# Cross attentions: scores for the maxima three heads earlier, rounding of q and k one pair earlier

## The chip, the core and the metric

The kernel runs on one core of a Trainium2 chip. The core has five engines with a queue each: PE (matrix products, with PEld as its weight loads), DVE (vectors), ACT (activations), POOL (GpSimd) and SP, which here only issues DMAs. Each queue is worked off in the order in which it was written; engines wait for each other on semaphores. The metric is the device time of one execution in microseconds, lower is better.

## The reference, cut to what matters

A decoder of two layers over x (64 sequences, 64 tokens, 256 channels). Stage by stage: a RWKV mixer, a banded cross attention with a context, a ternary MLP, a causal attention, a second cross attention without weights, and a mixture of experts. The change touches the two cross attentions alone. The first is:

```python
qkv = x @ w_in.T + b_in            # per sequence, 64 channels x 256 positions
scores = jnp.einsum('bqhd,bkhd->bhqk', q, k) / jnp.sqrt(jnp.asarray(d, q.dtype))
scores = jnp.where(band[None, None], scores, neg)      # |i - j| <= 64
attn = jax.nn.softmax(scores, axis=-1)
o = jnp.einsum('bhqk,bkhd->bqhd', attn, v).reshape(n, t, e)
o = o @ w_out.T + b_out
y = jax.nn.relu(o) * encodings
out = jnp.einsum('nit,io->not', y, w_ct) + b_ct[None, :, None]
```

The second has no projections, no band and no gate: its queries are the normalised x, its keys and values are the context itself, in 8 heads of 8 channels over 256 positions.

## The kernel before

`wide_attention` (L292) builds both cross attentions; `banded` tells the first from the second. Two sequences form a pair, so there are 32 pairs of 16 heads: heads 0 to 7 are those of the first sequence (s = 0), 8 to 15 of the second (s = 1). Each engine has one function `step(p, u, first, last)` that is written out 32 times, once per pair, with a loop over the heads j = 0 to 15 in it. Buffers alternate with the pair's parity u. What one head j of step p holds on PE:

- `make_scores_t` (L488, in the first attention with L491, which adds the band): transposed scores of pair p, two heads ahead (RING = 2). ACT takes their exponentials (L747).
- `make_scores` (L475): scores of pair **p + 1**, head j, for the row maxima alone. DVE takes the maxima (L617 in the first, L621 in the second). A score needs the maxima of two heads before it, as its bank in PSUM is shared by every second head.
- `multiply` (L506) at odd j, `align` (L516) of pair p - 1 at j = 4, and the small products of the first attention: `project` (L525, L526: q and k of pair p + 2) at j = 2, `make_values` (L535, in the second L541) at j = 5, `gate_product` (L554) at 10, `out_product` (L558) at 13.

The maxima go back into the transposed scores as three more rows of q. POOL splits them into three bf16 parts (`split_maxima`, L827 to L833), PE turns them (`turn_maxima`, L549: s = 1 of pair p at j = 1, s = 0 of pair p + 1 at j = 9), ACT copies them (`keep_maxima`, L780), and SP stores them with one DMA (`place_maxima`, L437: `xattn_qp<-xattn_mrow`). `make_scores_t` of heads 0 and 8 waits for that DMA (`rows_in`).

q and k are rounded to bf16 in three parts: ACT (`round_1`, L770), POOL (`left_overs`, L818), ACT (`round_2`, L774), POOL (L820). In step p this is done for pair p + 2, from j = 2 or 3 on. SP writes the parts to HBM (`store`, L416 and L420, six DMAs) and reads them back in the layout of the scores (`place`, L432, four DMAs for each s). SP's order in step p is: place_maxima(p, 1), store(p + 2), place(p + 2, 0), place_maxima(p + 1, 0), place(p + 2, 1), load_context. What sets each engine's order is the order of these calls in the code; nothing reorders it.

## Time and profile before

| | us |
|---|---|
| median of 3 runs | 2892.37 (2889.06 to 2894.8) |
| profiled execution, own time | 2875.17 |
| its span | 2873.3 |
| first cross attention: first to last score for the maxima | 391.7 to about 1098 |
| second cross attention: the same | 1869 to 2447 |
| PE busy over the span | 2247.8 (78%) |
| DVE, ACT, POOL busy over the span | 1850.9 (64%), 1165.6 (41%), 896.5 (31%) |

The page gives one profiled execution. In a timeline a row is: start, duration, engine, line, operation, output and inputs; a bracket at its end gives the time that the engine was idle before it and what ended that.
### The profile page before, as it was taken

How to read it: one execution, taken by the hardware profiler on the slowest of the kernel's cores; microseconds unless marked ns; L12 is line 12 of the kernel's file. 1: busy time of each engine (PE TensorE's matmuls, PEld its weight loads, DVE VectorE, ACT ScalarE, POOL GpSimd, SP SyncE). 2: the span in 40 equal slices, each digit the busy share in tenths (PEclk: the TensorE clock that was granted, in tenths of full speed). 3: DMA queues.
4: the chain of work that ended last, by engine and by line, in shares of the span. 5: the costliest groups of instructions: out<-in, count | busy, mean ns of one | idle time of the engine just before them, and what ended most of it. 6: DMA issues, size and time to landing. Idle time of an engine off the chain costs nothing. (4 is left out here: it accounts for less than half of the span.)

```text
span 2873.3 us, 55107 instructions
## 1 busy us (share of the span) xinstructions
PE 2247.8 (78%) x19084; PEld 1596.6 (56%) x19084; DVE 1850.9 (64%) x5654; ACT 1165.6 (41%) x2616; POOL 896.5 (31%) x1488
## 2 busy tenths in 40 slices
PE   4777658888888885599986999478888888549886
PEld 3666535555555553599975777334444444425553
DVE  4999956766666666655543666467777777415345
ACT  1222224444444443222224666246565655313222
POOL 3555622222222121466660000212222222143522
PEclk9888769999999897799997999779999999669998
DMA  3000042333223330000003000343333433022434
GB/s 106 1 1 0 1 114 74 85 79 81 74 74 85 78 82 4 1 2 2 2 16 130 2 2 1 109 93 101 92 102 93 102 92 86 7 83 76 145 119 155
DMA packets 252306, 183.17 MB, mean 64 GB/s; under 512 B 29056, under 2 KB 246304, under 8 KB 251264
## 3 DMA queue, kind: packets, MB, share of 16 engines
q1 hardware_dynamic: 240416, 156.52, 20.6%
q0 software_dynamic: 7456, 18.92, 1.8%
q10 hardware_dynamic: 4160, 4.19, 0.5%
q8 instruction: 157, 2.57, 0.4%
q14 instruction: 117, 0.96, 0.1%
HBM read 94.47 MB, written 83.51 MB: 62 GB/s over the span
## 5 line engine op out<-in xcount | busy, mean ns | idle before, releaser
L747 ACT ACTIVATE xattn_pr<-ps 128x384 f32<-128x384 f32 (+1 forms) x1024 | 536.6, 543 | 467.5 <-PE ps L491 281.8
L488 PE MATMUL ps<-xattn_qp,xattn_kp 128*128 128x192 bf16 (+1 forms) x2048 | 428.8, 270 | 93.6 <-DMA xattn_qp<-xattn_mrow 92.7
L475 PE MATMUL ps<-xattn_kp,xattn_qp 96*128 96x192 bf16 (+1 forms) x2048 | 386.7, 272 | 78.3 <-DVE xattn_mx L621 32.9
L621 DVE TENSOR_REDUCE xattn_mx<-ps 128x2 f32<-128x512 f32 x512 | 335.7, 677 | 154.1 <-PE ps L475 148.2
L506 PE MATMUL ps<-xattn_pr,xattn_vs 128*32 128x256 f32 (+1 forms) x4096 | 318.6, 384 | 19.9 <-ACT xattn_o L752 19.8
L617 DVE CUSTOM_DVE_ANT_0 xattn_masked<-ps,xattn_band 128x192 bf16<-128x192 f32 x1024 | 325.2, 354 | 8.4 <-issue 5.8
L488 PEld LDWEIGHTS ps<-xattn_qp,xattn_kp 128*128 128x128 bf16 x2048 | 189.5, 100 | 242.8 <-DMA xattn_qp<-xattn_mrow 120.2
L475 PEld LDWEIGHTS ps<-xattn_kp,xattn_qp 96*128 96x128 bf16 x2048 | 189.2, 102 | 133.6 <-DVE xattn_mx L621 54.7
L491 PE MATMUL ps<-xattn_band,xattn_ident 128*128 128x192 bf16 x1024 | 225.6, 259 | 0.0
L978 PE MATMUL ps<-ffn_parts,gate_up_t 128*128 128x128 bf16 x3072 | 194.4, 221 | 2.1 <-DVE ffn_parts L1096 2.1
L978 PEld LDWEIGHTS ps<-ffn_parts,gate_up_t 128*128 128x128 bf16 x3072 | 184.2, 98 | 16.3 <-DVE ffn_parts L1096 2.5
L615 DVE MEMSET xattn_tick<- 128x1 f32 x512 | 30.2, 59 | 227.2 <-PE ps L475 221.1
L1580 PE MATMUL ps<-expert_gu,moe_xbt 128*128 x312 | 157.4, 629 | 8.1 <-issue 4.2
L1806 DVE SCALAR_TENSOR_TENSOR moe_tg<-moe_tanh,ps 128x256 f32<-128x256 f32 x78 | 32.8, 421 | 195.5 <-ACT moe_tanh L1661 195.5
L506 PEld LDWEIGHTS ps<-xattn_pr,xattn_vs 128*32 128x32 f32 x4096 | 83.5, 110 | 120.9 <-issue 83.1
L992 PE MATMUL ps<-proj_t,ffn_h 128*128 128x256 f32 x512 | 138.7, 394 | 0.5 <-DVE ffn_h L1087 0.5
L818 POOL TENSOR_TENSOR xattn_rest<-xattn_qk,xattn_parts 128x512 f32<-128x512 f32 x64 | 74.0, 1156 | 206.7 <-ACT xattn_parts L770 206.7
L198 POOL TENSOR_TENSOR xattn_rs<-x_stat,const_sb 128x1 f32<-128x1 f32 x64 | 12.2, 190 | 395.9 <-DVE x_stat L193 395.9
L638 DVE RECIPROCAL xattn_rden<-ps 128x128 f32<-128x128 f32 x128 | 120.9, 947 | 22.0 <-PE ps L516 22.0
L1873 POOL DMA_INDIRECT moe_rows_out<-rwkv_w,moe_to x78 | 75.2, 964 | 185.2 <-DVE rwkv_w L1816 174.5
L827 POOL TENSOR_TENSOR xattn_mparts<-xattn_mx,const_sb 128x16 bf16<-128x16 f32 x128 | 27.6, 216 | 330.7 <-DVE xattn_mx L621 242.2
L1049 ACT ACTIVATE ffn_tanh<-ps 128x256 f32<-128x256 f32 x128 | 49.1, 383 | 195.4 <-PE ps L978 195.4
(304 smaller groups left out, 4736.7 us busy)
## 6 DMA issues: line engine op xcount, KB each, us to landing
xattn_rows<-xattn_parts SPq DMA_DIRECT2D x128, 192.0 KB, 2.1
xattn_qp<-xattn_rows SPq DMA_DIRECT2D x256, 96.0 KB, 2.9
xattn_kp<-xattn_rows SPq DMA_DIRECT2D x256, 96.0 KB, 3.2
xattn_rows<-xattn_parts SPq DMA_DIRECT2D x128, 128.0 KB, 2.1
moe_rows_in<-region_zero SPq DMA_DIRECT2D x6, 1677.0 KB, 7.3
moe_xb<-moe_rows_in SPq DMA_DIRECT2D x78, 129.0 KB, 2.1
xattn_rows<-xattn_parts SPq DMA_DIRECT2D x128, 64.0 KB, 1.8
moe_row<-moe_rows_out SPq DMA_DIRECT2D x16, 512.0 KB, 8.3
```

The source lines that it names most:

```text
L475: mm = nc.tensor.matmul(ps[:, BANK_S + j % RING, mt * D:mt * D + width], qp[u][s][0:R_MAX, h, mt * P:(mt + 1) * P], kp[u][s][0:R_MAX, h, l ...
L488: mm = nc.tensor.matmul(out, kp[u][s][:, h, nt * P:(nt + 1) * P], qp[u][s][:, h, lo:lo + width], start=True, stop=not banded)
L491: mm = nc.tensor.matmul(out, ident16[:], band16[:, nt, :], start=False, stop=True)
L506: mm = nc.tensor.matmul(out, vs[u][:, QUAD * g + t, nt, :], pr[(QUAD * t + g) % (2 * QUAD)][:, nt, q], start=first, stop=(t % 2 == 1 and n ...
L617: ins = nc.vector.tensor_tensor_reduce(out=masked[:, mt, :], in0=ps[:, BANK_S + j % RING, mt * D:mt * D + WIN], in1=band16[:, mt, :], scal ...
L621: ins = nc.vector.tensor_reduce(mx[s][:, h * NT:(h + 1) * NT], ps[:, BANK_S + j % RING, :].rearrange("p (m n) -> p m n", m=NT), AX.X, ALU.max)
L638: nc.vector.reciprocal(rden[:, x], ps[:, BANK_N, D + half * P:D + (half + 1) * P]).then_inc(normal, 1)
L747: nc.scalar.activation(out, src, ACT.Exp, scale=HD ** -0.5).then_inc(exped, 1)
L978: mm = nc.tensor.matmul(ps[:, BANK_G + j % 2, o:o + P], w(j, n % NT, ft), row, start=(n == 0), stop=(n == len(rows) - 1))
L992: mm = nc.tensor.matmul(ps[:, bank, 0:D], h[j % 2][:, ft * P:(ft + 1) * P], down_w(j, ft), start=start and ft == 0, stop=stop and ft == 1)
L1580: mm = nc.tensor.matmul(ps[:, BANK_G + n % 2, :], xbt[n % 2][:, kt, :], gu[:, kt, bass.ds(e, 1), :].rearrange("p a f -> p (a f)"), start=( ...
L1873: g.indirect_dma_start(y_out[part], bass.IndirectOffsetOnAxis(ap=to[n % RB][:, 0:1], axis=0), yb[n % RB], None,).then_inc(sent[n % RB], 16)
```

## The change

1. `make_scores` and the maxima on DVE run three heads further ahead (LEAD = 3): step p makes heads 3 to 15 of pair p + 1 and heads 0 to 2 of pair p + 2. Pair 1's first three stand before the steps.
2. The maxima are turned and kept one head earlier: s = 1 at j = 0, s = 0 at j = 8.
3. Normalising, projecting and rounding q and k in step p are for pair p + 3, not p + 2, and stand later in the step: `project` at j = 10 in place of 2, `round_1` and `round_2` at 11 and 13 (second attention: 7 and 9) in place of 3 and 5 (2 and 4). Storing and placing remain for pair p + 2. Pair 2 is rounded before the steps.
4. `make_values` moves from j = 5 to j = 3, DVE's `values` from 7 to 4, `normalise_q` from 0 to 5 (second: 3), `reciprocal_sums` from 5 and 6 to 6 and 7.
5. POOL splits s = 0 of pair p + 1 first, then makes the left overs, then splits s = 1 of pair p + 1; `reciprocal_std` stays last. On SP `load_context` of the second attention stands behind the six stores, and a wait on `placed` two pairs back is added before them.

```diff
+    LEAD = 3
@@ store, on SP
                     sp.wait_ge(left_over, 2 * (p + 1))
+                    for s in range(S2):
+                        if p >= 2:
+                            sp.wait_ge(placed[u][s], by_parity(p - 2, u, 64))
@@ step, on SP
-                    if not banded and there(p + 2):
-                        load_context(p + 2, u)
                     place_maxima(p, u, 1)
                     if there(p + 2):
                         store(p + 2, u)
+                    if not banded and there(p + 3):
+                        load_context(p + 3, 1 - u)
+                    if there(p + 2):
                         place(p + 2, u, 0)
...
@@ project and make_values, on PE
-                    wait(pe, vo_ready, p - 1)
                     wait(pe, qk_ready, p)
-                    wait(pe, max_kept, run(p - 1, 0))
+                    wait(pe, max_kept, run(p - 2, 0) + 1)
...
-                    if not banded:
-                        wait(pe, max_kept, run(p, 0))
+                    wait(pe, max_kept, run(p, 0))
...
@@ step, on PE
-                        if not last:
-                            make_scores(p + 1, 1 - u, j)
+                        ahead = next_head(p + 1, 1 - u, j + LEAD)
+                        if there(ahead[0]):
+                            make_scores(*ahead)
...
-                        if j == 1:
+                        if j == 0:
                             turn_maxima(p, 1)
-                        if banded and j == 2 and there(p + 2):
-                            project(p + 2, u)
+                        if not last and j == 3:
+                            make_values(p + 1, 1 - u)
+                        if not last and j == 8:
+                            turn_maxima(p + 1, 0)
+                        if banded and j == 10 and there(p + 3):
+                            project(p + 3, 1 - u)
...
+                if banded:
+                    project(2, 0)
+                for j in range(LEAD):
+                    make_scores(1, 1, j)
                 for j in range(RING):
                     make_scores_t(0, 0, j)
@@ step, on DVE
-                        if not last:
-                            maxima(p + 1, j)
-                        if j == 0 and there(p + 2):
-                            normalise_q(p + 2, u)
-                        if j in (5, 6) and not first:
-                            reciprocal_sums(p - 1, j - 5)
-                        if j == 7 and not last:
+                        ahead = next_head(p + 1, 1 - u, j + LEAD)
+                        if there(ahead[0]):
+                            maxima(ahead[0], ahead[2])
+                        if j == 4 and not last:
                             values(p + 1, 1 - u)
+                        if j == (5 if banded else 3) and there(p + 3):
+                            normalise_q(p + 3, 1 - u)
+                        if j in (6, 7) and not first:
+                            reciprocal_sums(p - 1, j - 6)
@@ step, on ACT
-                        if j == 1:
+                        if j == 0:
                             keep_maxima(p, u, 1)
                         if j == 2 and not first:
                             keep_o(p - 1)
-                        if there(p + 2):
-                            if banded and j == 2:
-                                projections(p + 2, u)
-                            if j == (3 if banded else 2):
-                                round_1(p + 2, u)
-                            if j == (5 if banded else 4):
-                                round_2(p + 2)
-                        if j == 9 and not last:
+                        if j == 8 and not last:
                             keep_maxima(p + 1, 1 - u, 0)
+                        if there(p + 3):
+                            if banded and j == 10:
+                                projections(p + 3, 1 - u)
+                            if j == (11 if banded else 7):
+                                round_1(p + 3, 1 - u)
+                            if j == (13 if banded else 9):
+                                round_2(p + 3)
@@ step, on POOL
-                    split_maxima(p, 1)
-                    if there(p + 2):
-                        left_overs(p + 2, u)
                     if not last:
                         split_maxima(p + 1, 0)
+                    if there(p + 3):
+                        left_overs(p + 3, 1 - u)
+                    if not last:
+                        split_maxima(p + 1, 1)
                     if not first:
                         fin.reciprocal_std(nc, g, p - 1)
```

What now stands in a row, at three places. PE, first attention, heads 2 and 3 of a step, before: the scores for the maxima of head 2, the two projections, head 3, and the first four products with the values (`pr` are the exponentials, `vs` the values).

```order
L475 MATMUL ps<-xattn0_kp00,xattn0_qp00 128x192 x2
L525 MATMUL ps<-xattn0_xn1,wide_q 128x256
L526 MATMUL ps<-xattn0_xn1,wide_k 128x256
L488 MATMUL ps<-xattn0_qp10,xattn0_kp10 128x192
L491 MATMUL ps<-xattn0_band16,xattn0_ident16 128x192
L488 MATMUL ps<-xattn0_qp10,xattn0_kp10 128x192
L491 MATMUL ps<-xattn0_band16,xattn0_ident16 128x192
L475 MATMUL ps<-xattn0_kp00,xattn0_qp00 128x192 x2
L506 MATMUL ps<-xattn0_pr0,xattn0_vs1 32x256
```

The same engine with the change, heads 10 and 11 of a step (line numbers shift: L483 is `make_scores`, L496 and L499 `make_scores_t`, L532 and L533 the projections, L562 `gate_product`, L514 `multiply`).

```order
L483 MATMUL ps<-xattn0_kp01,xattn0_qp01 128x192 x2
L532 MATMUL ps<-xattn0_xn0,wide_q 128x256
L533 MATMUL ps<-xattn0_xn0,wide_k 128x256
L562 MATMUL ps<-xattn0_on,wide_out 128x256
L496 MATMUL ps<-xattn0_qp11,xattn0_kp11 128x192
L499 MATMUL ps<-xattn0_band16,xattn0_ident16 128x192
```

The projections have left the place between heads 2 and 3, ahead of the products that wait for ACT's copy of o, and stand behind head 10.

ACT, first attention, before: `keep_maxima` at head 1, then the copy of o (L752), the projections' copies and the first rounding among the exponentials.

```order
L780 ACTIVATE xattn0_mrow1<-ps 48x128
L747 ACTIVATE xattn0_pr4<-ps 128x2x192
L752 ACTIVATE xattn0_o<-ps 128x512
L758 ACTIVATE xattn0_qk0<-ps,wide_b_q 128x256
L759 ACTIVATE xattn0_qk0<-ps,wide_b_k 128x256
```

ACT with the change, heads 10 to 13 of a step and on to head 0 of the next (L775 and L776 copy the projections, L787 and L791 round, L764 are exponentials, L797 is `keep_maxima`).

```order
L775 ACTIVATE xattn0_qk0<-ps,wide_b_q 128x256
L776 ACTIVATE xattn0_qk0<-ps,wide_b_k 128x256
L764 ACTIVATE xattn0_pr5<-ps 128x2x192
L787 ACTIVATE xattn0_parts<-xattn0_qk0 128x2x256
L764 ACTIVATE xattn0_pr6<-ps 128x2x192
L764 ACTIVATE xattn0_pr7<-ps 128x2x192
L791 ACTIVATE xattn0_parts<-xattn0_rest 128x2x256
L764 ACTIVATE xattn0_pr0<-ps 128x2x192
L764 ACTIVATE xattn0_pr1<-ps 128x2x192
L764 ACTIVATE xattn0_pr2<-ps 128x2x192
L797 ACTIVATE xattn0_mrow1<-ps 48x128
```

The rounding now ends three exponentials ahead of the keeping of the later half's maxima.

POOL, first attention, before: the split of s = 1, the two left overs (L818, L820), and the split of s = 0.

```order
L833 TENSOR_TENSOR xattn0_mparts<-xattn0_mrest,xattn0_mparts 128x16
L818 TENSOR_TENSOR xattn0_rest<-xattn0_qk1,xattn0_parts 128x512
L820 TENSOR_TENSOR xattn0_parts<-xattn0_rest,xattn0_parts 128x2x256
L827 TENSOR_TENSOR xattn0_mparts<-xattn0_mx0,const_sb 128x16
L829 TENSOR_TENSOR xattn0_mrest<-xattn0_mx0,xattn0_mparts 128x16
```

POOL with the change: the left overs (L839, L841) come right before the split of s = 1 (`mx1`, from L848 on), and `reciprocal_std` (L198, L200) behind it.

```order
L839 TENSOR_TENSOR xattn0_rest<-xattn0_qk1,xattn0_parts 128x512
L841 TENSOR_TENSOR xattn0_parts<-xattn0_rest,xattn0_parts 128x2x256
L848 TENSOR_TENSOR xattn0_mparts<-xattn0_mx1,const_sb 128x16
L850 TENSOR_TENSOR xattn0_mrest<-xattn0_mx1,xattn0_mparts 128x16
L852 TENSOR_TENSOR xattn0_mparts<-xattn0_mrest,const_sb 128x16
L854 TENSOR_TENSOR xattn0_mparts<-xattn0_mrest,xattn0_mparts 128x16
L198 TENSOR_TENSOR xattn0_rs<-x_stat,const_sb 128x1
```

The left overs changed sides: they stood ahead of the split of s = 0 and stand now ahead of that of s = 1.

## Rows read from the trace of the kernel before

**Rows 1.** PE's waits, first attention, 420 to 1100: total us, times, longest.

```profile
PE ps L488 <- DMA xattn_qp<-xattn_mrow: 65.1, 30, 4.2
PE ps L549 <- POOL xattn_mparts L833: 26.7, 51, 1.7
PE ps L475 <- DVE xattn_mx L617: 21.4, 43, 0.9
PE ps L506 <- ACT xattn_o L752: 0.5, 1, 0.5
```

**Rows 2.** PE's waits, second attention, 1900 to 2450.

```profile
PE ps L475 <- DVE xattn_mx L621: 31.3, 60, 0.6
PE ps L488 <- DMA xattn_qp<-xattn_mrow: 26.3, 24, 5.6
PE ps L506 <- ACT xattn_o L752: 17.4, 30, 0.6
PE ps L549 <- POOL xattn_mparts L833: 9.3, 32, 0.5
```

**Rows 3.** SP's issues in one step of the first attention: start, us, line.

```profile
728.73 1.46 SPq L416 DMA_DIRECT2D xattn_rows<-xattn_parts  x3
...
733.45 1.36 SPq L432 DMA_DIRECT2D xattn_qp<-xattn_rows  x2
...
735.83 0.76 SPq L437 DMA_DIRECT2D xattn_qp<-xattn_mrow  x1
```

**Rows 4.** PE's timeline, the wait that ends this chain.

```profile
738.44 0.26 PE L488 MATMUL ps<-xattn_qp,xattn_kp 128*128 128x192 bf16 x1 [2.24 <-DMA xattn_qp<-xattn_mrow]
```

**Rows 5.** Windows: us; busy of PE, PEld, DVE, ACT, POOL; PEclk; DMA; GB/s.

```profile
432.68:1082.97 650.29, 542.95 (x5277) 369.32 (x5275) 432.14 (x2638) 304.34 (x665) 140.72 (x348) 0.94 0.32 79
...
740.00:743.00 3.00, 3.00 (x24) 1.70 (x20) 2.81 (x18) 0.98 (x2) 1.60 (x6) 0.50 0.29 36
```

**Rows 6.** PE's timeline, first attention: aligns of pairs 0, 4, 5, 29, a wait.

```profile
432.68 1.92 PE L516 MATMUL ps<-xattn_o,const_sb 128*128 128x256 f32 x8
...
521.66 1.92 PE L516 MATMUL ps<-xattn_o,const_sb 128*128 128x256 f32 x8
...
535.16 0.26 PE L488 MATMUL ps<-xattn_qp,xattn_kp 128*128 128x192 bf16 x1 [1.47 <-DMA xattn_qp<-xattn_mrow]
...
543.19 1.92 PE L516 MATMUL ps<-xattn_o,const_sb 128*128 128x256 f32 x8
...
1082.97 1.92 PE L516 MATMUL ps<-xattn_o,const_sb 128*128 128x256 f32 x8
```

**Rows 7.** PE's timeline, second attention: aligns of pairs 0, 11, 14, 29.

```profile
1909.65 1.89 PE L516 MATMUL ps<-xattn_o,const_sb 128*128 128x256 f32 x8
...
2110.17 1.89 PE L516 MATMUL ps<-xattn_o,const_sb 128*128 128x256 f32 x8
...
2161.79 1.89 PE L516 MATMUL ps<-xattn_o,const_sb 128*128 128x256 f32 x8
...
2435.00 1.89 PE L516 MATMUL ps<-xattn_o,const_sb 128*128 128x256 f32 x8
```

**Rows 8.** Groups by line over the whole span: count, busy us, mean ns.

```profile
L818 POOL TENSOR_TENSOR xattn_rest<-xattn_qk,xattn_parts 128x512 f32<-128x512 f32 x64 | 74.0, 1156 | 206.7 <-ACT xattn_parts L770 206.7
...
L770 ACT ACTIVATE xattn_parts<-xattn_qk 128x512 bf16<-128x512 f32 x64 | 40.6, 634 | 37.5 <-DMA xattn_qk<-in_ctx 27.0 <-DMA xattn_rows<-xattn_parts 10.4
...
L541 PE MATMUL ps<-const_sb,xattn_qk 128*128 128x128 f32 x64 | 14.2, 305 | 25.8 <-DMA xattn_qk<-in_ctx 25.8
```

**Rows 9.** POOL's timeline, one split of maxima, first and last operation.

```profile
730.59 0.21 POOL L827 TENSOR_TENSOR xattn_mparts<-xattn_mx,const_sb 128x16 bf16<-128x16 f32 x1 [1.89 <-DVE xattn_mx L617]
...
731.48 0.22 POOL L833 TENSOR_TENSOR xattn_mparts<-xattn_mrest,xattn_mparts 128x16 bf16<-128x16 f32 x1
```

**Rows 10.** DVE's normalising, first attention: ns shortest, median, longest.

```profile
L170 DVE TENSOR_SCALAR xattn_xn<-x_now,x_stat x32: 407/410/1965, 372.1 to 1057.5; 128x256 f32<-128x256 f32 x32
```

**Rows 11.** POOL's timeline at the start of the first attention.

```profile
372.01 7.60 POOL L845 MEMSET xattn_kp<- 128x2048 bf16 x4 [4.80 <-POOLq L206]
```

More of the change, by code:

```diff
@@ L460, in _ @@
                         place(p, p, s)
+                if not banded:
+                    load_context(2, 0)
                 place_maxima(0, 0, 0)
@@ L528, in make_values @@
                 def make_values(p, u):
-                    if not banded:
-                        wait(pe, max_kept, run(p, 0))
+                    wait(pe, max_kept, run(p, 0))
                     if banded:
-                        pe.wait_ge(qk_ready, p + 2 if there(p + 1) else p + 1)
+                        if p == 0:
+                            pe.wait_ge(qk_ready, 2)
                         for nt in range(NT):
@@ L548, in turn_maxima @@
                         pe.wait_ge(vo_ready, p + 1)
+                    elif banded and there(p + 2):
+                        pe.wait_ge(qk_ready, p + 3)
                     nc.tensor.transpose(ps[:, BANK_PREP, 0:P // 2].bitcast(BF16), mparts[:], ident16[:]).then_inc(max_turned, 1)
@@ L572, in step @@
                             align(p - 1)
-                        if j == 1:
+                        if j == 0:
                             turn_maxima(p, 1)
-                        if banded and j == 2 and there(p + 2):
-                            project(p + 2, u)
+                        if not last and j == 3:
[4 more added lines that the diff above has]
+                            project(p + 3, 1 - u)
                         if banded and not first and j == 10:
                             gate_product(p - 1)
-                        if not last and j == 5:
-                            make_values(p + 1, 1 - u)
                         if banded and not first and j == 13:
                             out_product(p - 1)
-                        if not last and j == 9:
-                            turn_maxima(p + 1, 0)
                 if banded:
@@ L727, in _ @@
                 values(0, 0)
+                normalise_q(2, 0)
                 for j in range(NHS):
                     maxima(0, j)
+                for j in range(LEAD):
+                    maxima(1, j)
                 over(v, PAIRS, step)
@@ L805, in _ @@
                 keep_maxima(0, 0, 0)
+                if banded:
+                    projections(2, 0)
+                round_1(2, 0)
+                round_2(2)
                 a.wait_ge(preset, 3)
@@ L850, in _ @@
                 split_maxima(0, 0)
+                left_overs(2, 0)
+                split_maxima(0, 1)
                 over(g, PAIRS, step)
```

## The prediction

> **What bounds the kernel now.** I read the waits of PE first, since the two cross attentions fill most of the profile's costly groups and PE is the engine with the largest busy time in both. In the first attention PE waits 65.1 us in 30 pairs for the DMA that stores the maxima's rows, 26.7 us for POOL's split of the maxima, 21.4 us for DVE's maxima, and once for ACT's copy of o [rows 1]. In the second the same list is shorter: 31.3 us for DVE, 26.3 for the DMA, 17.4 for the copy of o, 9.3 for the split [rows 2].
>
> Next, who makes that DMA late. The SP queue shows it: in one step the six stores of the rounded parts start at 728.73, the placing that has to wait for them to land at 733.45, and only behind it, at 735.83, the DMA of the maxima's rows [rows 3]. PE gets its rows at 738.44 after 2.24 us of idle time [rows 4]. The last operation of the split that belongs to this DMA started at 731.48 [rows 9], so the data was ready over 3 us before it could be issued: SP's queue is the cause, and what holds the queue is the rounding of q and k in the same step.
>
> Third, the pace. The reader counts from one align to another. In the first attention 29 periods lie between 432.68 and 1082.97: 650.29 / 29 = 22.42 us each [rows 6]. The granted clock is 0.94 over that stretch, against 0.50 (1.2 GHz) for 740 to 743, right behind the wait that ends at 738.44 [rows 4, 5]. A pair without such a stretch is 521.66 to 543.19, 21.53 us with a DMA wait of 1.47 in it [rows 6]. In the second attention 29 periods take 525.35 / 29 = 18.12 us, and the three from 2110.17 to 2161.79, in which PE hardly waited for the DMA, 51.62 / 3 = 17.21 [rows 7].
>
> **First attention, per pair.** Start from 21.53. (a) The rows' DMA: the store of pair p + 2 now finds its parts rounded a whole pair ago, so SP issues it right behind the maxima of head 0 instead of at a late left over. The six stores take about 3 us of issue, the first placing has to wait for head 5's transposed scores anyway, and the maxima of the earlier half are asked for at head 8 with SP's queue empty. From there to head 14 there are six heads, some 8 us at 21.53 / 16 = 1.35 each, for an issue and a landing that took 738.44 - 735.83 = 2.6 us [rows 3, 4]. The wait goes: -1.47. What is late next is not SP but the split of the later half, (c). (b) Half-speed stretches: 22.42 - 21.53 = 0.89 per pair is the clock and the longer DMA waits that come with it; the one in rows 5 begins behind such a wait, as those elsewhere in the stretch that I followed, so I let it go too. (c) The split: before, it cost PE 26.7 / 30 = 0.89 per pair in two waits. The earlier half's is made three heads before it is turned, so that one goes. The later half's stands behind the left overs of p + 3 on POOL, which stand behind ACT's second rounding at head 13. From that rounding: 0.63 (ACT) + 1.16 (POOL) + the split, 731.48 + 0.22 - 730.59 = 1.11, is 2.9 us [rows 8, 9]; it begins some 1.6 us into head 13 because the first left over (1.16) must be done, and PE reaches the turning at head 0 about 3.7 us after head 13 began. 1.6 + 2.9 - 3.7 = about 0.7 stays. That estimate is the weak one; nothing (0) and twice it (1.5) bound it. (d) DVE: the reciprocals come one head later and values leaves that stretch for head 4, so the queue of DVE behind the align is as long as before; I take 0.5 at heads 9 and 10, against 21.4 / 30 = 0.71 now. The wait at head 1 is covered by the turning's. (e) A new wait: in the first attention PE waited for ACT's copy of o once, because the projections of pair p + 2 stood between heads 2 and 3 and filled that time. They are gone to head 10. In the second attention, which never had them, the wait is 17.4 / 30 = 0.58 in each pair [rows 2]. I charge +0.58.
>
> Sum: 21.53 - 1.47 = 20.06; the split's 0.89 and DVE's 0.71 are in it on average, and that pair has them as 0.44 + 0.70 and 0.42 + 0.67, that is 2.23; 20.06 - 2.23 = 17.83 of work; + 0.7 + 0.5 + 0.58 = **19.6**. Against 22.42 that is -2.8 x 29 = **-82**. Bounds: with new waits of 1.0 in all 18.8 (-105), with all the old small waits kept beside the new one 20.6 (-53).
>
> **Second attention, per pair.** No projections, so no (e). The clean pace is 17.21; -0.91 against 18.12 is what the DMA wait is worth. But from the align to the score of head 13 DVE works without a break, and PE waits for it at heads 9 and 13 (31.3 / 30 = 1.04 per pair) [rows 2]. DVE loses values there and keeps maxima, reciprocals and the new x, and starts on the reciprocals a head later, so the score of head 13 comes as long after the align as before. The two transposes of make_values (L541, 0.305 each, overlapping to about 0.3) stood inside this stretch and cost nothing; at head 3 they stand ahead of the align and are on the path: +0.3 [rows 8]. The earlier half's split wait (9.3 / 30 = 0.31) lay in the same stretch and gives nothing back. 17.21 + 0.3 = **17.5**, -0.6 x 29 = **-18**. Bounds 17.0 (-32) and 18.3 (+5). Rounding at heads 7 and 9 needs the context that SP now loads behind the stores, at about head 4; it needs about 3 us to land and ACT asks at head 7, so this is just covered.
>
> **Ends of the stages.** In the first attention the longest DMA wait, 4.2 us in the first step, and its half-speed stretch go [rows 1]; against that pair 2 is rounded before the first exponentials: two roundings and two left overs, 2 x 0.63 + 2 x 1.16 = 3.6 [rows 8], and a split of 1.1, about +5. The second has a wait of 5.6 to lose [rows 2] and pays the same chain less what its own first maxima hide. I take -3 and -7: **-10**. The added wait on SP (placed, two pairs back) is for DMAs that landed a pair ago and what is queued behind it, six stores, never feels it; its cost is 0. The other stages keep their code.
>
> **Sum.** -82 - 18 - 10 = -110. Against the profiled execution that is 2875.17 - 110 = 2765; its time lies 17.2 below the median, and against the median of 2892.37 it is **2782**.
>
> **A rule that speaks against it.** DVE's normalising of one tile takes 0.407 us at the shortest and 1.965 at the longest [rows 10]; the long ones begin at 372.1, while POOL runs four memsets of 7.60 / 4 = 1.9 each [rows 11]. So a DVE operation can be held for a whole POOL operation. The Trainium skill says so in "SBUF — State Buffer", section "SBUF: two separate sides": DVE and GpSimd share one pair of ports as an exclusive lock, which also concerns DVE operations with two inputs in SBUF, and the loser waits for the whole instruction. By that rule, the trace agrees for memsets; no row shows it for the left overs, which stood beside no such DVE operation. Leaving it out gives 2782, and rival 1 is what it would make of the same sum.
>
> **Rivals.**
> 1. *DVE held by the left overs.* In the second attention the new x (two inputs in SBUF) is due at head 10 in DVE's unbroken stretch, and the second left over now follows a rounding at head 9. If it is hit in every pair, 1.16 x 29 = 34 us come back: 2782 + 34 = 2816. For: rows 10 and 11. Against: by the sums above the left over ends just before the new x begins, and an operation that starts second on POOL costs DVE nothing. 0.12.
> 2. *The half-speed stretches stay.* If they have another cause than the DMA waits, 0.89 x 29 = 26 us stay: 2808. For: the clock also fell behind waits of under 2 us. Against: at 740 the fall stands right behind a wait of 2.24, and with those gone the waits left are those of 0.6 and less that the clean pairs have too. 0.10.
> 3. *The change doesn't do what it says*: the rows' wait moves to head 6, since the later half's DMA stands behind the placing that waits for head 13's transposed scores. Then only the clock, the split and the ends move: of 82 + 18 about 35 remain, 2892 - 45 = 2847. Against: that placing takes about 2 us and is over before head 0. 0.08.
> 4. *Slower: the later half's chain lies bare.* At head 0 PE waits for the two copies of the projections (each of half a rounding's elements, so 0.63 together, an estimate from rows 8), rounding (0.63), left over (1.16), rounding, left over and split (1.11): 5.3 us if ACT gets to none of it while PE works on heads 10 to 15. Then it is (5.3 - 0.7) x 29 = 133 more, 2782 + 133 = 2915. It decides from a wait of 0.7 + 110 / 29 = 4.5 us. For: exponentials stand between all of these on ACT. Against: ACT is busy 304 of 650 us [rows 5]. 0.06.
>
> **How the numbers follow.** Forecast 0.60, between about 2760 and 2806; rivals 0.12, 0.10, 0.08, 0.06; 0.04 for a still larger gain. The range takes in the forecast, rivals 1 and 2 and the bounds of the first attention as far as they are likely: 2752 to 2828, 0.82. A measurement of this kernel can tell about 0.2% (5.8 us) from no change. Faster: 0.60 + 0.12 + 0.10 + 0.08 + 0.01 = 0.91; the same 0.03; slower 0.06.
>
> **What would show it.** In the changed profile: align to align 19.6 us and 17.5 us; the wait for the maxima's DMA gone from PE's list in both; a wait for the copy of o near 0.58 in each pair of the first attention; one split wait per pair, at head 0, near 0.7; PEclk at 1.00 in the first attention; SP's stores right behind the maxima of head 0. I am wrong if the first attention's pace is above 20.6, if DVE's new x in the second is longer than its 0.4, or if the split's wait at head 0 is over 1.5.

## The result

The changed kernel takes 2773.97 us (median of 4, 2772.57 to 2778.94) against 2893.59 for the kernel before (the three executions of the table and a fourth); the ratio is 0.9588 with a 95% interval of 0.9566 to 0.961, that is 119.6 us less. The forecast was 2782, 110 less than 2892.37. One execution of one of the later versions (*spread*, below) took 8234.72 us at a granted clock of 0.494; it is in no ratio and no median here.

The profiled execution of after took 2778.94 us (span 2776.9). Read in the order of the prediction, the waits of PE come first; total us, times, longest. The first attention, 420 to 1020:

```profile
PE ps L483 <- DVE xattn_mx L630: 32.2, 89, 0.6
PE ps L514 <- ACT xattn_o L769: 15.7, 31, 0.8
PE ps L566 <- DVE xattn_y L667: 8.9, 28, 0.3
PE ps L557 <- POOL xattn_mparts L854: 1.2, 1, 1.2
```

The second, 1820 to 2350:

```profile
PE ps L483 <- DVE xattn_mx L634: 36.1, 89, 0.5
PE ps L514 <- ACT xattn_o L769: 19.2, 31, 1.0
PE ps L557 <- POOL xattn_mparts L854: 0.3, 1, 0.3
```

The DMA of the maxima's rows (65.1 and 26.3 us in [rows 1, 2]) is on neither list, and the split is down to a single wait in each. What is left is DVE, the copy of o, and one entry that [rows 1] don't have: out_product waits for y.

SP's issues in one step of the first attention, start and us:

```profile
724.42 0.73 SPq L442 DMA_DIRECT2D xattn_qp<-xattn_mrow  x1
725.26 1.46 SPq L421 DMA_DIRECT2D xattn_rows<-xattn_parts  x3
726.77 1.43 SPq L425 DMA_DIRECT2D xattn_rows<-xattn_parts  x3
731.21 0.81 SPq L437 DMA_DIRECT2D xattn_qp<-xattn_rows  x2
732.06 0.93 SPq L437 DMA_DIRECT2D xattn_kp<-xattn_rows  x2
734.47 0.73 SPq L442 DMA_DIRECT2D xattn_qp<-xattn_mrow  x1
```

Against [rows 3] the stores follow the rows of the later half at once, and the rows of the earlier half (734.47) find an empty queue.

The windows from the align of pair 0 to that of pair 29, columns as in [rows 5]:

```profile
434.55:1002.56 568.01, 513.08 (x5276) 350.91 (x5275) 447.36 (x2638) 297.69 (x663) 135.15 (x346) 1.00 0.35 89
1827.37:2326.86 499.49, 443.06 (x4062) 242.47 (x4061) 399.41 (x723) 311.38 (x608) 135.04 (x346) 1.00 0.36 101
```

568.01 / 29 = 19.59 us per pair against 22.42 [rows 6], 499.49 / 29 = 17.22 against 18.12 [rows 7]; single periods are 19.62 and 17.22 nearly without exception. PEclk is 1.00 where it was 0.94 [rows 5]. So 650.29 - 568.01 = 82.3 us come from the first attention and 525.35 - 499.49 = 25.9 from the second.

The ends give nothing. The start is 1.9 later, the stretch from align 29 of the first attention to align 0 of the second 1.9 shorter, and what lies behind align 29 of the second attention is 450.0 us long against 438.3. Apart from the last two pairs that is code that wasn't changed. The window behind the last align of before, and then that of after:

```profile
2461.41:2873.30 411.89, 289.69 (x1216) 186.96 (x1216) 174.51 (x556) 102.88 (x302) 137.49 (x144) 0.83 0.32 102
```

```profile
2351.80:2776.90 425.10, 289.77 (x1216) 187.38 (x1216) 175.19 (x556) 102.33 (x302) 137.59 (x144) 0.83 0.31 99
```

The same instructions, the same busy time on PE (289.7 and 289.8) and the same clock, 13 us apart. In the twelve traces of the experiments the part behind align 29 is 442 to 452 us, so the one execution of before that was profiled had a short end; it also lies 18 us below the median of its kernel, and that of after 5 above its own. So the two profiled executions differ by 96 us and the medians by 120. The short end accounts for about 9 of these 24 us; where in the program the rest lies isn't known, as before has one trace.

### The profile page after: what moved, and what is told of

Its sections match the earlier page's. It is cut to its first block and busy times, and to the rows that moved or that the text cites. A ratio compares the mean times of both kernels' runs of the same rounds, so it can differ in the third digit from the quotient of the medians.

```text
span 2776.9 us, 55137 instructions
## 1 busy us (share of the span) xinstructions
PE 2217.8 (80%) x19084; PEld 1573.4 (57%) x19084; DVE 1868.5 (67%) x5654; ACT 1154.9 (42%) x2616; POOL 892.0 (32%) x1488
## 5 line engine op out<-in xcount | busy, mean ns | idle before, releaser
L764 ACT ACTIVATE xattn_pr<-ps 128x384 f32<-128x384 f32 (+1 forms) x1024 | 544.3, 542 | 459.6 <-PE ps L499 260.0
L483 PE MATMUL ps<-xattn_kp,xattn_qp 96*128 96x192 bf16 (+1 forms) x2048 | 375.0, 265 | 99.1 <-DVE xattn_mx L634 38.3
L496 PE MATMUL ps<-xattn_qp,xattn_kp 128*128 128x192 bf16 (+1 forms) x2048 | 412.0, 263 | 3.3 <-ACT xattn_pr L764 2.7
L514 PE MATMUL ps<-xattn_pr,xattn_vs 128*32 128x256 f32 (+1 forms) x4096 | 307.2, 372 | 35.1 <-ACT xattn_o L769 34.9
L496 PEld LDWEIGHTS ps<-xattn_qp,xattn_kp 128*128 128x128 bf16 x2048 | 178.7, 97 | 171.7 <-issue 91.1
L483 PEld LDWEIGHTS ps<-xattn_kp,xattn_qp 96*128 96x128 bf16 x2048 | 175.5, 99 | 176.7 <-DVE xattn_mx L630 60.6
L499 PE MATMUL ps<-xattn_band,xattn_ident 128*128 128x192 bf16 x1024 | 211.2, 247 | 0.0
L839 POOL TENSOR_TENSOR xattn_rest<-xattn_qk,xattn_parts 128x512 f32<-128x512 f32 x64 | 74.0, 1156 | 340.8 <-ACT xattn_parts L787 340.8
L848 POOL TENSOR_TENSOR xattn_mparts<-xattn_mx,const_sb 128x16 bf16<-128x16 f32 x128 | 27.6, 215 | 459.0 <-DVE xattn_mx L634 277.7
L514 PEld LDWEIGHTS ps<-xattn_pr,xattn_vs 128*32 128x32 f32 x4096 | 82.7, 108 | 132.6 <-issue 66.6
L1995 PE MATMUL ps<-rwkv_xt,rwkv_w_now 128*128 128x256 f32 x384 | 122.8, 404 | 4.8 <-DVE rwkv_w L2075 3.0
L524 PE MATMUL ps<-xattn_o,const_sb 128*128 128x256 f32 x512 | 122.1, 381 | 1.4 <-ACT xattn_o L769 1.4
```

The lines of the kernel that those rows point to most:

```text
L483: mm = nc.tensor.matmul(ps[:, BANK_S + j % RING, mt * D:mt * D + width], qp[u][s][0:R_MAX, h, mt * P:(mt + 1) * P], kp[u][s][0:R_MAX, h, l ...
L496: mm = nc.tensor.matmul(out, kp[u][s][:, h, nt * P:(nt + 1) * P], qp[u][s][:, h, lo:lo + width], start=True, stop=not banded)
L499: mm = nc.tensor.matmul(out, ident16[:], band16[:, nt, :], start=False, stop=True)
L514: mm = nc.tensor.matmul(out, vs[u][:, QUAD * g + t, nt, :], pr[(QUAD * t + g) % (2 * QUAD)][:, nt, q], start=first, stop=(t % 2 == 1 and n ...
L524: mm = nc.tensor.matmul(ps[:, BANK_N, sums * D:(sums + 1) * D], c[:, at:at + P], o_sb[:, half, :], start=(half == 0), stop=(half == 1))
L764: nc.scalar.activation(out, src, ACT.Exp, scale=HD ** -0.5).then_inc(exped, 1)
```

## Experiments: what the change consists of

Ratios are to the kernel before on the same chip, whose median there was 2889.4 to 2895.66. Differences in us between two versions can be between chips, so one of a few us says nothing. A pace is the time from the align of pair 0 to that of pair 29, divided by 29, from the profiled execution.

**sp_order.** The kernel before with two lines exchanged on SP.

```
                         store(p + 2, u)
-                        place(p + 2, u, 0)
                     if not last:
                         place_maxima(p + 1, 1 - u, 0)
                     if there(p + 2):
+                        place(p + 2, u, 0)
                         place(p + 2, u, 1)
```

> The kernel before, with one thing changed on SP: the DMA of the earlier half's rows is issued ahead of the placing of pair p + 2 instead of behind it. Rounding, storing and scores stay where they were. Queue theory: the rows were ready at about 732.5 and stood 3 us behind the placing, so PE's wait of 65.1 us in the first attention and 26.3 in the second falls under 0.3 per pair, the half-speed stretches behind those waits go too, the first attention's pace is 20.1 instead of 22.42 and the second's 17.3 instead of 18.12; total about 2893 - 67 - 24 = 2800. Rival A (the late stores hold the queue whatever stands behind them): a wait of 1 us or more stays and the pace is 21 or more, total above 2830. Rival B (half-speed stretches have another cause): the wait goes, but some 60 us or more at 0.50 stay between the aligns of the first attention, total about 2826.

Measured: 2796.59 us, ratio 0.9669 (0.9651 to 0.9687). Paces 19.98 and 17.66. PE's waits in the first attention, 420 to 1100:

```profile
...
PE ps L549 <- POOL xattn_mparts L833: 33.0, 57, 1.7
PE ps L475 <- DVE xattn_mx L617: 20.6, 46, 0.9
PE ps L475 <- DMA xattn_kp<-xattn_rows: 14.2, 19, 2.3
...
PE ps L488 <- DMA xattn_qp<-xattn_mrow: 0.4, 1, 0.4
```

65.1 us of waiting have become 0.4, and the granted clock is 1.00 over 430.16 to 1009.62. What came new is a wait for the placing (14.2), which now goes last. The queue theory held: the order of two lines alone gives four fifths of the gain of the whole change (ratio 0.9669 against 0.9588).

**round_only.** The changed kernel without the lead: `LEAD = 0`, turnings at heads 1 and 9, the later half's split first on POOL.

> The changed kernel with the scores for the maxima no further ahead than before (LEAD 0, turnings at heads 1 and 9, the later half's split ahead of the earlier half's on GpSimd); rounding and storing stay shifted by a pair. Theory: the shift of the rounding carries most of the gain, since it alone frees SP's queue. The waits for the rows' DMA stay away; the split's waits come back as before, 0.89 per pair in the first attention and 0.31 in the second: paces 20.5 and 17.5, total about 2774 + 26 + 9 = 2809. Rival (scores ahead carry the gain): paces back at 22 and 18, total above 2860.

Measured: 2810.94, ratio 0.9709 (0.9692 to 0.9725). Paces 20.67 and 17.29. Waits from 430 to 1030:

```profile
PE ps L483 <- DVE xattn_mx L630: 33.2, 58, 0.9
PE ps L557 <- POOL xattn_mparts L854: 28.8, 58, 0.7
PE ps L514 <- ACT xattn_o L769: 14.3, 29, 0.5
PE ps L566 <- DVE xattn_y L667: 8.9, 28, 0.3
```

No DMA is on the list. Shifting the rounding removes the cause but is 14 us slower than *sp_order*: it also takes the projections away from between heads 2 and 3, which opens the wait for o (0.49 per pair), and puts a left over beside y, which opens the one for y (0.32; y takes 1.07 us here against 0.43 in *sp_order*, and why is said further down). These are 23 us in this list, and DVE's maxima cost 33.2 where they cost 20.6 there, against 14.2 for the placing there. The lead, with the earlier turnings and POOL's new order, is worth 2810.94 - 2773.97 = 37 us, nearly all of it in the first attention (1.09 per pair against 0.07).

**lead_only.** The kernel before with `LEAD = 3`, turnings at heads 0 and 8, rounding and storing where they were.

> The kernel before with scores three heads ahead and the turnings at heads 0 and 8, but with rounding and storing of pair p + 2 where they were. Theory: the first score of pair p + 2 is now asked for at head 13, and its placing, issued from 733.45 to 735.78 in the step of rows 3, lands about 2 us later, while PE is at head 13 at about 734.9: a wait of some 3 us for the placing (qp or kp) takes the place of the one for the rows' DMA. Pace in the first attention 22 to 23.5 with half-speed stretches still there, total 2880 to 2930. Rival: the lead alone removes the split's waits and the placing comes in time: pace about 21.5, total below 2860.

Measured: 2925.98, ratio 1.0092 (1.0062 to 1.0122): 0.9% slower than before. Paces 23.53 and 18.72. From 420 to 1140:

```profile
PE ps L476 <- DMA xattn_kp<-xattn_rows: 89.0, 30, 4.6
PE ps L550 <- DVE xattn_vs L680: 37.3, 30, 1.3
```

The wait for the rows has been replaced by one for the placing, 3.0 per pair; the second row I had not foreseen: the turning writes into the bank from which DVE's `values` read, and at head 8 it has to wait for those of head 7 (1.24 per pair); the changed kernel has them at head 4. Neither half of the change does what both do together: the lead needs the placing early, and only the shifted rounding gives it that.

**lead2.** The changed kernel with `LEAD = 2`.

> The changed kernel with scores for the maxima two heads ahead instead of three; the turnings stay at heads 0 and 8. Theory: in the first attention the split of the later half stands behind the left overs on GpSimd and not behind the maxima, so one head less costs nothing there, and the earlier half's split ended 2.6 us ahead of its turning (711.49 against 714.14 in the trace of after): pace 19.6. In the second the split would end some 0.4 us behind the turning at head 8, of which the DVE queue hides a part: pace 17.2 to 17.5. Total 2772 to 2785. Rival: the gain of the lead (37 us between the changed kernel and the one with no lead) is spread evenly over its three heads: 2774 + 12 = 2786 with a longer pace in the first attention too, 20.0.

Measured: 2774.75, ratio 0.9593 (0.9565 to 0.9621); paces 19.64 and 17.22. No difference from three heads in the total; single periods of the first attention are 19.68 against 19.62. The third head buys nothing here, which fits that the split stands behind the left overs and not behind the maxima.

## Experiments: the clock and the bare chain

**rows_behind.** The changed kernel; on SP `place_maxima(p + 1, 1 - u, 0)` goes behind `place(p + 2, u, 1)`.

> The changed kernel with one thing moved on SP: the DMA of the earlier half's rows is issued behind the placing of pair p + 2's later half, so that PE has to wait for it at head 14. By rows 3: 2.0 us of issues from the scores of head 13 on, then 2.6 us from issue to landing, less about 1.3 that PE works meanwhile: a bare wait of 3.3 us per pair. Theory (the clock falls behind such waits): half-speed stretches come back in both attentions, and the pace is 19.62 + 3.3 + about 1 = 24 in the first; total about 2774 + 58 x 3.3 + 30 to 60 = 3000 to 3025. Rival (the stretches had another cause): PEclk stays at 1.00 between the aligns and the pace is 22.9, total about 2965.

Measured: 3063.26, ratio 1.058 (1.0562 to 1.0598). Paces 23.86 and 22.64. First PE's wait, in 430 to 1140 and in 1960 to 2617, then the windows of both:

```profile
PE ps L496 <- DMA xattn_qp<-xattn_mrow: 99.1, 30, 4.4
...
PE ps L496 <- DMA xattn_qp<-xattn_mrow: 91.1, 29, 3.4
```

```profile
439.46:1131.50 692.04, 557.95 (x5277) 381.30 (x5275) 450.31 (x2638) 300.13 (x663) 135.11 (x346) 0.92 0.27 73
1960.56:2617.10 656.54, 509.48 (x4062) 264.08 (x4061) 403.93 (x723) 318.27 (x608) 135.08 (x346) 0.88 0.27 76
```

The wait had the predicted size (3.3 and 3.1 per pair), and the clock that was 1.00 in both attentions of after is 0.92 and 0.88. So such waits bring the clock down, and the rival is out. The total came out above the expected 3000 to 3025 because the clock's part was underrated: 0.08 x 2 x 692 = 111 us at half speed in the first, 0.12 x 2 x 657 = 158 in the second. In the second the pace rose by 22.64 - 17.22 = 5.4. The wait is 3.1 of it; the other 2.3 stand beside 158 / 29 = 5.4 us per pair at half speed. By this estimate about 0.4 us is lost for each us at 1.2 GHz.

How long must PE stand still? No single length tells. Two waits of the kernel before, and the windows right behind them:

```profile
447.79 0.26 PE L488 MATMUL ps<-xattn_qp,xattn_kp 128*128 128x192 bf16 x1 [3.00 <-DMA xattn_qp<-xattn_mrow]
...
760.31 0.34 PE L488 MATMUL ps<-xattn_qp,xattn_kp 128*128 128x192 bf16 x1 [1.80 <-DMA xattn_qp<-xattn_mrow]
```

```profile
447.79:452.79 5.00, 3.63 (x44) 2.42 (x45) 3.88 (x24) 1.96 (x4) 1.72 (x6) 1.00 0.45 68
760.31:765.31 5.00, 4.73 (x40) 3.19 (x40) 3.36 (x21) 1.96 (x4) 1.57 (x6) 0.66 0.41 72
```

Behind 3.00 us the clock stays at 2.4 GHz, behind 1.80 it is at 1.2 for a part of the next 5 us. In the second attention of *lead_only* it falls behind 1.96 (2080.91) and not behind 1.85 (2062.20). In *sp_order*, with the DMA waits gone, there is one half-speed stretch between the aligns of the first attention, behind two short waits that follow each other:

```profile
944.28 0.34 PE L475 MATMUL ps<-xattn_kp,xattn_qp 96*128 96x192 bf16 x2 [0.87 <-DVE xattn_mx L617]
...
945.79 0.23 PE L549 MATMUL ps<-xattn_ident,xattn_mparts 128*128 128x128 bf16 x1 [0.70 <-POOL xattn_mparts L833]
```

```profile
945.79:950.79 5.00, 5.00 (x32) 3.22 (x33) 1.50 (x12) 3.09 (x8) 0.76 (x1) 0.66 0.01 2
```

The Trainium skill (TensorE: Matmul & The Clock Gate, Part 1) says that the granted clock follows how busy PE has been recently. The trace agrees: the stretches come and go with PE's waits, and not with the length of the last one alone.

**chain_late.** The changed kernel with projections at head 12 and roundings at heads 13 and 15 in the first attention, the mechanism of rival 4.

> The changed kernel with the chain of pair p + 3 in the first attention two heads later: projections at head 12, roundings at heads 13 and 15. The second attention is unchanged. Theory (the slower rival of the forecast, that the later half's chain can lie bare, needs only such a shift): in the trace of after GpSimd's split ends at 743.35 and PE turns at 743.40, so there is no slack; two heads are about 2.5 us, and PE waits about 2.5 us at head 0 in each pair, with a half-speed stretch behind some of the waits: pace 22 to 23 in the first attention, 17.22 in the second, total about 2774 + 31 x 2.5 to 3.4 = 2850 to 2880. Rival: slack on ACT and GpSimd that the two end points don't show takes up most of it: wait under 1 us, total below 2805.

Measured: 2862.32, ratio 0.9891 (0.9863 to 0.9918). Paces 22.54 and 17.22. From 430 to 1100:

```profile
PE ps L557 <- POOL xattn_mparts L854: 69.5, 29, 2.9
```

One of these waits, the end of POOL's split and PE's turning:

```profile
749.83 0.22 POOL L854 TENSOR_TENSOR xattn_mparts<-xattn_mrest,xattn_mparts 128x16 bf16<-128x16 f32 x1
...
750.11 0.29 PE L557 MATMUL ps<-xattn_ident,xattn_mparts 128*128 128x128 bf16 x1 [2.38 <-POOL xattn_mparts L854]
```

The window from align to align:

```profile
439.31:1092.83 653.52, 567.29 (x5276) 383.56 (x5275) 432.48 (x2638) 299.40 (x663) 134.32 (x346) 0.91 0.30 77
```

2.4 us in each pair, and the clock down to 0.91. Two heads later and three quarters of the gain are gone: the version that was timed stands right at the edge. In the trace of after these rows are the scores and the turning at head 8, then the end of POOL's split, the scores and the turning at head 0:

```profile
733.60 0.33 PE L483 MATMUL ps<-xattn_kp,xattn_qp 96*128 96x192 bf16 x2
733.77 0.22 PE L557 MATMUL ps<-xattn_ident,xattn_mparts 128*128 128x128 bf16 x1
...
743.13 0.22 POOL L854 TENSOR_TENSOR xattn_mparts<-xattn_mrest,xattn_mparts 128x16 bf16<-128x16 f32 x1
```

```profile
743.17 0.33 PE L483 MATMUL ps<-xattn_kp,xattn_qp 96*128 96x192 bf16 x2
743.40 0.23 PE L557 MATMUL ps<-xattn_ident,xattn_mparts 128*128 128x128 bf16 x1
```

The data is ready at 743.35, PE comes at 743.40. That isn't slack. In *chain_late*, where PE plainly waits, it also comes 0.06 behind the split's end (750.05 and 750.11). And at head 0 the turning starts 0.23 behind the scores ahead of it; at head 8, where the split had ended 2.66 us before, it starts 0.17 behind them. So PE is released by the split in after as well: 0.06 us in each pair, which no list of waits shows, since the matmuls overlap.

## Experiments: the waits that are left

**o_first.** The changed kernel; on ACT the copy of o goes ahead of the exponential of head 2.

```
                     for j in range(NHS):
+                        if j == 2 and not first:
+                            keep_o(p - 1)
                         ahead = next_head(p, u, j + RING)
```

> The changed kernel with ACT's copy of o at head 2 ahead of the exponential of the same head instead of behind it. Theory: the wait for that copy (15.7 us in 31 in the first attention, 19.2 in 31 in the second, in the trace of after) is on the path in every pair, and ACT has 1.28 us of idle time ahead of that exponential, so the copy costs nothing there: paces 19.62 - 0.5 = 19.1 and 17.22 - 0.6 = 16.6, total about 2774 - 15 - 18 = 2741. Rival: in the second attention DVE bounds the stretch and the gain there is given back as a longer wait at head 13; only the first gains, total about 2759.

Measured: 2731.77, ratio 0.9444 (0.9418 to 0.9471); paces 19.02 and 16.55. The wait is gone in both attentions. On ACT the copy now starts when the product is done, out of idle time:

```profile
660.85 0.60 ACT L769 ACTIVATE xattn_o<-ps 128x512 f32<-128x512 f32 x1 [0.86 <-PE ps L514]
```

**values_first.** The changed kernel; on PE `make_values` at head 3 goes ahead of `multiply(0)`.

> The changed kernel with make_values at head 3 ahead of multiply(0) instead of behind it. It covers the same wait for the copy of o instead of removing it: in the first attention its matmuls take 0.44 us between two others on PE, in the second about 0.3. Theory: gain of 0.44 and 0.3 per pair, paces 19.2 and 16.9, total about 2774 - 13 - 9 = 2752. Rival (the two transposes were hidden anyway, which would also explain why the pace of the second attention shows no sign of the 0.3 that the forecast put there): no gain in the second, total about 2761.

Measured: 2750.08, ratio 0.9514 (0.9488 to 0.954); paces 19.05 and 16.96. In the second attention 0.26 per pair is gained, so the two transposes stood on the path there, as the prediction said.

**x_late.** The changed kernel; DVE's new x and statistics of pair p - 2 at head 4 behind values, out_product at head 14, POOL's reciprocal of the deviation a step later.

> The changed kernel with DVE's new x and its statistics (0.48 + 0.43 + 0.18 us in the first attention, 0.41 + 0.43 + 0.18 in the second) moved a step later, to head 4 behind values, where DVE has over 1 us of idle time in both attentions, and out_product from head 13 to head 14. Theory: PE's waits for DVE's maxima are the queue behind those operations: in the first attention the wait at head 1 (0.53) and the one of out_product for y (0.32) go, in the second the wait at head 13 (0.55) goes: paces 18.8 and 16.7, total about 2774 - 25 - 16 = 2733. Rival: the waits only move to another head, since DVE is the bound from the align on; total above 2755.

Measured: 2733.55, ratio 0.9457 (0.9428 to 0.9486); paces 18.96 and 16.52. The waits at head 1 and for y are gone (out_product comes a head later; y still takes 1.07); one of 0.45 at head 13 came new in the first attention. In the second PE waits 16.5 us for DVE from 1830 to 2230 instead of 28.5.

**both.** *o_first* and *x_late* together.

> The copy of o ahead of the exponential and the late new x together. Theory: the two waits lie at different places of a pair and add up: paces 18.3 and 16.1, total about 2774 - 33 - 41 = 2700. Rival: they share the same slack (DVE's queue behind the align), and the sum is less than the two single gains: above 2715.

Measured: 2692.85, ratio 0.9315 (0.929 to 0.9341); paces 18.39 and 15.84. The single gains were 42.2 and 40.4, their sum 82.6; together 81.1. They add up.

**y_apart.** *both* with `gate_by_context`, which makes y, at head 12 instead of 11.

> The version with the early copy of o and the late new x, with one thing changed: DVE's reading of the gate's product and the making of y at head 12 instead of 11. In the trace of that version y (two inputs in SBUF) starts at 721.01, 0.37 after GpSimd's left over of 720.64 to 721.81, and takes 1.07 us; in the kernel before, where no left over is near, it takes 0.43. Theory: the left over holds y, y holds the maxima behind it on DVE, and these make PE wait 0.45 at head 13. A head later y falls between the two left overs: it takes 0.43, the wait goes, the pace of the first attention is 18.0 instead of 18.43 and the total about 2693 - 13 = 2680; the second attention stays at 15.84. Rival: the two reciprocals in a row are what PE waits for at head 13 too, as at head 9; y gets short, but the wait and the pace stay: 2693.

Measured: 2697.31, ratio 0.9333 (0.9306 to 0.936); paces 18.34 and 15.84. The first half of the theory held, the second fell. The duration of y (line 667; shortest, median, longest ns), in *both* and then in *y_apart*:

```profile
L667 DVE TENSOR_TENSOR xattn_y<-xattn_gate,xattn_ctx x32: 425/1074/1076, 444.5 to 998.5; 128x256 f32<-128x256 f32 x32
```

```profile
L667 DVE TENSOR_TENSOR xattn_y<-xattn_gate,xattn_ctx x32: 424/425/436, 446.4 to 998.7; 128x256 f32<-128x256 f32 x32
```

y is short again and the wait at head 13 is gone, but y comes later by itself, and out_product waits 0.24 for it; 0.05 per pair is left, and the total is no better than that of *both*.

**spread.** *both* with the reciprocals at heads 6 and 8, the normalised o at 9, the gate's product at 11 and its reading at 12.

> The version with the early copy of o and the late new x, with DVE's two reciprocals at heads 6 and 8 instead of 6 and 7, the normalised o at head 9, the gate's product at head 11 and its reading at head 12. Theory: the waits for DVE that are left (0.36 at head 9 in both, 0.45 at head 13 in the first, 0.31 at head 11 in the second) are the queue behind two reciprocals of 0.95 in a row: at least half of them go, paces 18.0 and 15.5, total about 2693 - 12 - 10 = 2671. Rival: DVE is the bound from the align on whatever the order, and the same waits come a head later: 2685 to 2700.

Measured: 2670.26 (2670.16 to 2675.72), ratio 0.9239 (0.9204 to 0.9273); paces 18.01 and 15.56. Waits from 420 to 1000:

```profile
PE ps L483 <- DVE xattn_mx L630: 11.6, 32, 0.4
PE ps L566 <- DVE xattn_y L667: 8.7, 31, 1.1
```

DVE costs PE 11.6 us where it cost 32.2 in after. This version beats both kernels: 222 us below before, 104 below the changed kernel. It differs from the changed kernel only in where eight calls stand.

## Why the prediction was right, and where it was not

*SP's queue.* Right, and shown by *sp_order* and *rows_behind* from both sides. The Trainium skill (DMA: Bandwidth & Descriptors, "Anatomy of one DMA — SWDGE (gpsimd) path") says that a wait for a semaphore happens on the issuing sequencer. The trace agrees for SP as the issuer: the rows' DMA, ready over 3 us before, was issued at 735.83, behind the placing that had waited until 733.45 [rows 3].

*The clock, (b).* Right: PEclk 1.00, and 0.92 and 0.88 once such a wait is back. Rival 2 fell. What it held for itself is true: the clock also fell behind waits under 2 us.

*The split, (c).* Forecast 0.7, measured 0.06. The estimate let the second rounding begin 1.6 us into head 13; it began at 740.42, 1.1 behind the first product of that head at 739.28, because ACT's first rounding comes only one exponential behind its copies of the projections. And PE reached the turning 4.1 us into that head instead of 3.7, since it had waited for y. The chain from the rounding on was 2.93 as forecast (2.9). So 1.1 + 2.9 - 4.1 leaves the chain and PE meeting almost to the point.

*DVE, (d).* Forecast 0.5, measured (in PE's timeline, in nearly every pair) 0.36 + 0.19 at heads 9 and 10 and 0.53 at head 1, which I took to be covered by the turning's wait. With that wait gone, nothing covered it.

*y.* Not foreseen: 0.32 per pair. Rival 1 named the mechanism and looked for it in the wrong place. Two rows of after, DVE and POOL:

```profile
739.60 1.07 DVE L667 TENSOR_TENSOR xattn_y<-xattn_gate,xattn_ctx 128x256 f32<-128x256 f32 x1
```

```profile
739.23 1.16 POOL L839 TENSOR_TENSOR xattn_rest<-xattn_qk,xattn_parts 128x512 f32<-128x512 f32 x1 [8.12 <-ACT xattn_parts L787]
```

y has two inputs in SBUF and starts 0.37 into a left over; it ends at 740.67, 0.28 after it, and takes 1.07 instead of the 0.43 of the kernel before. In *chain_late*, *y_apart* and *spread*, where no left over is under way when y starts, it takes 0.43 again. The rule of the Trainium skill (SBUF — State Buffer, "SBUF: two separate sides"), that the engine that comes second is blocked, agrees with this in kind; in size y lost 0.64 of the 0.79 us that the left over still ran. It was to be checked for every DVE operation beside the moved left overs, and not for the new x of the second attention alone, which keeps its 0.41.

*The copy of o, (e).* Forecast 0.58, measured 0.49.

The terms 0.7 + 0.5 + 0.58 = 1.78 stand against 0.06 + 0.36 + 0.19 + 0.53 + 0.32 + 0.49 = 1.95, and 17.83 of work against 19.62 - 1.95 = 17.67. The mechanism, a free queue on SP and a clock that stays up, was right; that the pace was right to 0.02 (-82 against -82.3) is luck, since the split, the copy of o and the work were too high and DVE and y too low by as much.

*The second attention.* 17.5 forecast, 17.22 measured. The 0.3 of make_values was right (*values_first*: 0.26). What I missed are two small gaps of before: in the period from 2144.57, PE's next product started 0.77 behind the multiply at 2158.35, which has the turning behind it, and 0.70 behind the one at 2155.11, where 0.57 is usual. In after the turning stands between two scores and pushes the next by 0.06. 0.2 - 0.06 + 0.13 = 0.27 pays for make_values. The first part comes with the turning's new place; what made the second gap no run tells.

*The ends.* -10 forecast, nothing measured in the two traces; the longest waits of the first steps did go, and the added prologue cost as much. Of the 119.6 by the medians, the two attentions account for 108 in the traces; for the other 11 no trace shows a place, and the one profiled execution of before lies 18 below its median.

*Rival 3* didn't happen: no wait at head 6. *Rival 4* didn't, but the chain had no slack at all. Its chance of 0.06 was too low for a slack that my own sum put below zero. The chances don't add up either: the list gives 0.94 for faster (the 0.04 for a still larger gain is left out of the 0.91) and nothing for the same.

## What to carry to other kernels

Before a pipeline is deepened, try whether the one late transfer can be issued ahead of what waits in its queue: here that alone gave four fifths of the gain. When work is moved out of a gap, look at what it covered; the waits opened here (o, y, the maxima at head 1) were removed by moving one call in *o_first* and three in *x_late*, and the gains added up. A chain whose end already releases its reader is a risk, even if the wait is only 0.06 us and in no list: two heads of delay cost 88 us.

## What the runs showed of the hardware

- Half-speed stretches of PE came behind stops of 1.7 us and more (1.71 at 513.63 and 1.80 at 760.31 in before), and once behind two of 0.87 and 0.70 close together (*sp_order*), while a stop of 3.00 (447.79 in before) had none behind it. Each us at 1.2 GHz cost about 0.4 us, an estimate from *rows_behind*.
- A DVE operation with two inputs in SBUF that started 0.37 into a POOL operation on SBUF ended 0.28 behind its end: 1.07 us for 0.43, in 28 of 32 pairs. The other way round POOL gave way less: in *spread* a left over that started 0.19 before the end of y took 1.21 instead of 1.16.
- PE's turning started 0.06 us behind the end of the POOL operation that released it, both with a wait of 2.38 in the list (*chain_late*) and with none (after).
- Behind a product of o and a turning (2158.35 in before) the next score came 0.2 us later than usual; a turning between two scores pushed the next by 0.06. Of the 0.2, 0.13 also stood behind a product without a turning (2155.11), so their cause is open.
